# A three-layer feature-interaction kernel on one core: field pairs on partitions in place of transposed products

## The chip, the cores and the metric
The kernel runs on one core of a Trainium2 chip. The metric is device time in microseconds (us) of one execution. A core has TensorE (PE in the profile; its weight loads are PEld), VectorE (DVE), ScalarE (ACT), GpSimd (POOL), SyncE (SP), which here only issues transfers, and 16 DMA engines. Each engine works through its own instructions in order and waits on semaphores that the others raise.

## The reference
A batch of 1024 samples has 39 fields; each field looks up a row of 16 values and a bias, scaled by the sample's feature value. Three interaction layers follow, all per sample b and embedding component d, and then two dense layers on the 624 scaled inputs:

```python
inputs = emb[feature_ids] * feature_vals[:, :, None]          # 1024 x 39 x 16
h = inputs
for i in range(3):
    x = jnp.einsum('bhd,bmd->bhmd', h, inputs).reshape(B, -1, EMB_DIM)
    x = jax.nn.relu(jnp.einsum('bcd,oc->bod', x, Ws[i]) + bs[i][None, :, None])   # 200 outputs
    if i != 2: h, direct = (x[:, :100], x[:, 100:])
    else: direct = x
    finals.append(direct)
cin_result = jnp.sum(jnp.concatenate(finals, axis=1), axis=-1)
d = relu(relu(inputs.reshape(B, -1) @ dnn_W0.T + dnn_b0) @ dnn_W1.T + dnn_b1)    # 624 -> 400 -> 400
out = concatenate((cin_result, d)) @ fc_W.T + fc_b + sum(input_biases)
```

Layer 0 has 780 products per sample and component (symmetric pairs merged), layers 1 and 2 have 100 x 39 = 3900 each.

## The kernel before
The batch is 8 tiles of 128 samples; a tile and one of the 16 components make a chunk, so there are 128 chunks (`CHUNKS`). In a chunk the products of a layer are the contraction of a matmul: 7 tiles of 128 products in layer 0, 31 in layers 1 and 2 each (`KT`). Each value is split into a high part that the one-pass matmul format holds and a low part, and a tile is multiplied as high x (weights high, weights low), 400 columns, and low x (weights high), 200 columns (`multiply_group`, L524 and L525). One group of four tiles in layers 1 and 2 is not split and multiplied in full precision instead (L516).

GpSimd forms the products with samples on the partitions (L397 for layer 0, L414 for layers 1 and 2, 3900 elements in four pieces each). The matmul wants products on the partitions, so every group of four tiles is turned first: TensorE turns those of layer 0 (L496), VectorE transposes blocks of 32x32 for the others (`turn_group`, L719), out of an order of weights and inputs that makes 32x32 blocks enough. ScalarE rounds a turned group to its high part (`high`, L582), VectorE subtracts (`low`, L725), TensorE multiplies. The layer's sum is put together by ScalarE (`low_copy`, L589) and VectorE (`add`, L735), dotted with the final weights (`dot`, L742), and its first 100 outputs are copied, quarter by quarter, as the next layer's h (`quarter`, L598, 16 small ACTIVATEs a layer).

A step i (function `step`, written out by hand; a hardware loop runs over most of them) works on layer 0 of chunk i+1, layer 1 of chunk i and layer 2 of chunk i-1. GpSimd also gathers the embedding rows of the next tile, one indirect DMA for each field (`gather`, L364; two or three at the head of each step, by `gathers(j)`), and scales them once a tile (`scale`, L374 to L385). After the last chunk the dense layers run tile by tile (L530 to L532, L757, L763).

## Time and profile before

| | us |
|---|---|
| median of 3 runs (lowest, highest) | 3019.55 (3016.03, 3020.39) |
| the profiled execution | 3024.12 |
| its span, from first to last instruction | 3022.3 |
| mean granted TensorE clock | 0.996 of full |

Busy shares of the span: PE 95%, PEld 92%, DVE 90%, POOL 80%, ACT 72%. Busy time counts each instruction from start to end, and neighbours on one engine overlap by up to a third, so a share near 90% may still hide idle time: the distance between the starts of two neighbours is what an engine spends on one. A wait is read from the brackets of a row of the timeline: idle time, and what ended it.

### The profile page before, as it was taken

How to read it: one execution, taken by the hardware profiler on the slowest of the kernel's cores; microseconds unless marked ns; L12 is line 12 of the kernel's file. 1: busy time of each engine (PE TensorE's matmuls, PEld its weight loads, DVE VectorE, ACT ScalarE, POOL GpSimd, SP SyncE). 2: the span in 40 equal slices, each digit the busy share in tenths (PEclk: the TensorE clock that was granted, in tenths of full speed). 3: DMA queues.
4: the chain of work that ended last, by engine and by line, in shares of the span. 5: the costliest groups of instructions: out<-in, count | busy, mean ns of one | idle time of the engine just before them, and what ended most of it. 6: DMA issues, size and time to landing. Idle time of an engine off the chain costs nothing.

```text
span 3022.3 us, 69958 instructions
## 1 busy us (share of the span) xinstructions
PE 2883.5 (95%) x18848; PEld 2783.5 (92%) x18848; DVE 2731.5 (90%) x5355; ACT 2163.4 (72%) x6593; POOL 2417.9 (80%) x1513
## 2 busy tenths in 40 slices
PE   0799999999999999999999999999999999999998
PEld 0799999999999999999999999999999999999997
DVE  2699999999999999999999999999999999999995
ACT  2677777777777777777777777777777777777772
POOL 7788888888888888888888888888888888767660
PEclk9899999999999999999999999999999999999999
DMA  6100010000000010000100001000100001000001
GB/s 122 19 1 1 1 22 1 1 1 7 16 1 1 1 22 1 1 1 1 22 1 1 1 1 22 1 1 1 21 2 1 1 1 22 1 0 0 0 35 30
DMA packets 36455, 29.42 MB, mean 10 GB/s; under 512 B 22960, under 2 KB 28976, under 8 KB 36400
## 3 DMA queue, kind: packets, MB, share of 16 engines
q1 hardware_dynamic: 26160, 26.11, 3.8%
q0 software_dynamic: 10240, 2.81, 3.2%
q14 instruction: 48, 0.39, 0.0%
q8 instruction: 7, 0.11, 0.0%
HBM read 26.33 MB, written 2.56 MB: 10 GB/s over the span
## 4 chain that ended last, share of the span: by engine, by line
ACT 30%; issue 29%; DVE 29%; PE 6%; DVEq 2%; ACTq 2%; POOL 2%; DMA 1%; SPq 0%; POOLq 0%
DVE xlo L725 15%; ACT h2q L598 10%; ACT h1q L598 10%; ACT xhi L582 10%; DVE turn L719 7%; DVE acc_sum L735 4%; PE acc L524 2%; DVE x_whole L719 2%; POOL raw L364 1%; DVEq L723 1%; ACTq L580 1%; PE acc L525 1%; DVE spent L742 1%; PE turn L496 1%; PE acc L516 1%
## 5 line engine op out<-in xcount | busy, mean ns | idle before, releaser
L524 PE MATMUL acc<-W,xhi 128*128 128x400 f32 x7808 | 2437.0, 374 | 61.3 <-DVE xlo L725 36.0
L525 PE MATMUL acc<-W,xlo 128*128 128x200 f32 x7808 | 1990.3, 255 | 0.0
L524 PEld LDWEIGHTS acc<-W,xhi 128*128 128x128 f32 x7808 | 1467.5, 188 | 154.5 <-DVE xlo L725 153.5
L725 DVE TENSOR_TENSOR xlo<-turn,xhi 128x512 fp32r<-128x512 f32 (+1 forms) x2088 | 1341.7, 648 | 223.7 <-ACT xhi L582 194.6
L525 PEld LDWEIGHTS acc<-W,xlo 128*128 128x128 f32 x7808 | 1492.1, 191 | 0.0
L582 ACT ACTIVATE xhi<-turn 128x512 fp32r<-128x512 f32 (+1 forms) x2088 | 1165.4, 571 | 397.9 <-PE acc L525 216.2
L414 POOL TENSOR_TENSOR prods<-h1q,xq 128x1092 f32<-128x1092 f32 (+2 forms) x512 | 933.1, 1854 | 413.7 <-ACT h1q L598 407.2
L719 DVE STREAM_TRANSPOSE turn<-prods 128x512 f32<-128x512 f32 (+1 forms) x1792 | 1244.9, 695 | 18.3 <-POOL prods L414 13.3
L414 POOL TENSOR_TENSOR prods<-h2q,xq 128x1092 f32<-128x1092 f32 (+2 forms) x512 | 934.1, 1854 | 12.6 <-ACT h2q L598 12.6
L598 ACT ACTIVATE h1q<-acc_sum 32x25 f32<-32x25 f32 x2048 | 456.2, 223 | 242.5 <-DVE acc_sum L735 215.1
L598 ACT ACTIVATE h2q<-acc_sum 32x25 f32<-32x25 f32 x2048 | 456.9, 223 | 76.9 <-DVE acc_sum L735 49.6
L516 PE MATMUL acc<-w_whole,x_whole 128*128 128x200 f32 x2048 | 393.0, 335 | 0.0
L364 POOL DMA_INDIRECT raw<-table,idx x320 | 313.4, 979 | 89.4 <-issue 82.3
L516 PEld LDWEIGHTS acc<-w_whole,x_whole 128*128 128x128 f32 x2048 | 336.4, 190 | 0.0
L397 POOL TENSOR_TENSOR prods<-xin 128x780 f32 (+1 forms) x128 | 215.5, 1684 | 5.2 <-POOL idx L359 3.1
L496 PE MATMUL turn<-ident,prods 128*128 128x128 f32 (+1 forms) x928 | 146.0, 275 | 69.1 <-POOL prods L397 67.8
L589 ACT ACTIVATE acc_lo<-acc 128x200 f32<-128x200 f32 x384 | 129.2, 337 | 96.7 <-PE acc L525 96.7
L719 DVE STREAM_TRANSPOSE x_whole<-prods 128x512 f32<-128x512 f32 x256 | 177.3, 693 | 0.0
L496 PEld LDWEIGHTS turn<-ident,prods 128*128 128x128 f32 (+1 forms) x928 | 105.6, 141 | 71.7 <-issue 68.3
L735 DVE TENSOR_TENSOR acc_sum<-acc,acc_lo 128x200 f32<-128x200 f32 x384 | 135.2, 352 | 10.4 <-ACT acc_lo L589 10.4
L742 DVE SCALAR_TENSOR_TENSOR spent<-acc_sum,fcp 128x100 f32<-128x100 f32 (+1 forms) x384 | 105.5, 275 | 0.1
L742 DVE DVE_READ_ACCUMULATOR spent<-acc_sum,fcp (+1 forms) x384 | 32.6, 85 | 0.0
(44 smaller groups left out, 227.5 us busy)
## 6 DMA issues: line engine op xcount, KB each, us to landing
xq<-x_store SPq DMA_DIRECT2D x32, 312.0 KB
raw<-table,idx POOLq DMA_INDIRECT x320
prods<-w SPq DMA_DIRECT2D x9, 500.0 KB, 7.8
x_store<-xin SPq DMA_DIRECT2D x8, 312.0 KB
raw<-x_store SPq DMA_DIRECT2D x8, 312.0 KB, 2.9
prods<-d SPq DMA_DIRECT2D x1, 1000.0 KB, 4.8
w_whole<-w SPq DMA_DIRECT2D x2, 400.0 KB, 12.8
prods<-d SPq DMA_DIRECT2D x1, 800.0 KB, 6.5
```

The costliest lines, as they stand in the source:

```text
L364: nc.gpsimd.indirect_dma_start(out=raw[:, m * EMB_COLS:(m + 1) * EMB_COLS], out_offset=None, in_=table, in_offset=bass.IndirectOffsetOnAxi ...
L397: nc.gpsimd.tensor_tensor(prods[:, 0:PAIRS].rearrange("p (s a) -> p s a", a=FIELDS), x[:, 0:FIELDS].unsqueeze(1).broadcast_to([P, SHIFTS, ...
L414: nc.gpsimd.tensor_tensor(out[:, :, a * FIELDS:b * FIELDS].rearrange("p q (h m) -> p q h m", m=FIELDS), hq[layer - 1][:, :, a:b].unsqueeze ...
L496: mm = pe.transpose(turn[slot][0:rows, at:at + P], src[:, t * P:t * P + rows], ident[:])
L516: mm = pe.matmul(bank[:, 0:OUTS], x_whole[:, job - 1, at:at + P], w_whole[:, job - 1, t % GROUP, :], start=False, stop=False, skip_group_c ...
L524: pe.matmul(bank[:, 0:2 * OUTS], hi, w, start=start, stop=end, skip_group_check=True)
L525: mm = pe.matmul(bank[:, 0:OUTS], lo, w[:, 0:OUTS], start=False, stop=end, skip_group_check=True)
L582: op = nc.scalar.activation(xhi[0:rows, slot, cols], turn[slot][0:rows, cols], ACT.Copy)
L598: op = nc.scalar.activation(hq[layer][QUARTER * i:QUARTER * (i + 1), q, :], acc_sum[QUARTER * q:QUARTER * (q + 1), layer, H_QUARTER * i:H_ ...
L719: nc.vector.transpose(place.rearrange("p (t q s) -> p t q s", q=4, s=QUARTER), src.rearrange("p q (t k) -> p t q k", k=QUARTER)).then_inc( ...
L725: op = nc.vector.tensor_tensor(xlo[0:rows, slot, cols], turn[slot][0:rows, cols], xhi[0:rows, slot, cols].bitcast(F32), ALU.subtract)
L735: nc.vector.tensor_tensor(acc_sum[:, layer, :], acc[layer][:, 0:OUTS], acc_lo[:, layer, :], ALU.add).then_inc(s_acc[layer], 1)
```

## The change
Samples move to the columns and products to the partitions, so that no product is transposed. In layers 1 and 2 a tile is one field m (31 of them) with 96 of the h rows on partitions 0 to 95; the remaining 8 fields and 4 h rows fill partitions 96 to 127. SyncE copies the inputs of a chunk out of DRAM onto all partitions that need them (`load_block`, four blocks a chunk; `load_layer0`), and h is turned once a layer by TensorE (`turn`, one 128x128 transpose) and then spread by ScalarE to its places in PSUM (`hrep`, for VectorE) and in SBUF (`hrep_s`, for GpSimd) by six ACTIVATEs (`spread`).

The groups of four tiles of a step are 6 P groups, whose products and low parts are GpSimd's, and 12 D groups, whose products and low parts are VectorE's. ScalarE makes the high parts of both. `ORDER` gives the order in which TensorE multiplies them and ScalarE rounds them. P0 and P1 are layer 0 (4 and 3 tiles), P2, P3 and D0 to D5 are layer 1, P4, P5 and D6 to D11 layer 2; D5 and D11 have three tiles, the last of which holds high and low part in one operand and needs a single 400-column matmul. Both GpSimd and VectorE form the product of the next group just before the subtraction of the present one. Every product tile is split; the full-precision group is gone. GpSimd's gathers stay at the head of its step (`gathers(j)`, ahead of `step`; none at j = 7, where `scale` stands).

Each tile of 128 samples, the scaled inputs are turned by VectorE (`turn_inputs`), stored to DRAM by 8 transfers (`store_inputs`) and copied into further layouts by 22 (`spread_inputs`). The weights are reordered at the start through DRAM (`load_weights`) and split between steps -1, 0 and 1 (`split_weights`). The dense layers read their inputs already turned. The core of the diff:

```diff
+ORDER = [("P", 0), ("D", 0), ("D", 1), ("P", 1), ("D", 2), ("D", 3), ("P", 2), ("D", 4), ("D", 5), ("P", 3),
+         ("D", 6), ("D", 7), ("P", 4), ("D", 8), ("D", 9), ("P", 5), ("D", 10), ("D", 11)]
 LAST = CHUNKS - 1
...
+PRING, DRING, BANKS = 3, 4, 3
...
+def layer_of(kind, g):
+    return g // 2 if kind == "P" else 1 + g // 6
+def tiles_of(kind, g):
+    if kind == "P":
+        return range(GROUP * (g % 2), min(GROUP * (g % 2) + GROUP, KT[0] if g < 2 else KT[1]))
+    return range(2 * GROUP + GROUP * (g % 6), min(3 * GROUP + GROUP * (g % 6), KT[1]))
+def present(i):
+    if not isinstance(i, int):
+        return (0, 1, 2)
+    return tuple(n for n in range(3) if 0 <= i + 1 - n <= LAST)
...
+            def store_inputs(tile):
+                sp.wait_ge(s_xt, tile + 1)
+                waited()
+                for q in range(4):
+                    for j, n in ((0, QUARTER), (1, M_ALL - QUARTER)):
+                        sp.dma_start(
+                            xs[bass.ds(tile * DIM, DIM), QUARTER * j:QUARTER * j + n,
+                               QUARTER * q:QUARTER * (q + 1)].rearrange("d c b -> c d b"),
+                            xt[QUARTER * q:QUARTER * q + n, :, j, :]).then_inc(s_xs, 16)
...
+            def spread_inputs(tile):
+                sp.wait_ge(s_xs, tile * 128 + 128)
+                waited()
+                to = xe[bass.ds(tile * DIM, DIM), :, :, :]
...
+            def step(i, buf):
+                if not isinstance(i, int) or i + 2 <= LAST:
+                    sp.wait_ge(s_prod_p, p_num(i, 1) + 1)
+                    waited()
+                    load_layer0(i + 2)
+                full = 2 in present(i)
+                if full:
+                    sp.wait_ge(s_prod_d, d_num(i, 7) + 1)
+                    waited()
+                load_block(i + 1, buf, 1)
+                if full:
+                    sp.wait_ge(s_prod_d, d_num(i, 9) + 1)
+                    waited()
+                load_block(i + 1, buf, 2)
+                if full:
+                    sp.wait_ge(s_prod_p, p_num(i, 5) + 1)
+                    waited()
+                load_block(i + 1, buf, 0)
+                if full:
+                    sp.wait_ge(s_prod_d, d_num(i, 11) + 1)
+                    waited()
+                load_block(i + 1, buf, 3)
+            load_weights(1, w1)
+            store_inputs(0)
+            spread_inputs(0)
+            load_layer0(0)
...
+            step(1, 0)
+            with sp.Fori(0, TILES - 1) as k:
+                for j in range(DIM):
+                    if j == 9:
+                        store_inputs(k + 1)
+                    if j == 10:
+                        spread_inputs(k + 1)
+                    if j == 12:
+                        sp.wait_ge(s_xe, (k + 2) * (16 * XE_DMAS))
+                        waited()
+                    step(k * DIM + (j + 2), (j + 1) % 2)
...
+            def product(i, par, k):
+                n, layer, tiles = p_num(i, k), layer_of("P", k), tiles_of("P", k)
+                if k == 0:
+                    pool.wait_ge(s_l0x, (i + 2) * 96)
+                elif k == 2:
+                    pool.wait_ge(s_hrep[0], i + 1)
+                    pool.wait_ge(s_xblk[0], (i + 1) * 32)
+                elif k == 4:
+                    pool.wait_ge(s_hrep[1], i)
+                if some(n - 2):
+                    pool.wait_ge(s_lo_p, n - 2)
+                a, count = tiles[0], len(tiles)
...
+            def low(i, k):
+                n, slot, cols = p_num(i, k), p_slot(i, k), len(tiles_of("P", k)) * P
+                pool.wait_ge(s_hi_p, n + 1)
+                nc.gpsimd.tensor_tensor(xlo_p[:, slot, 0:cols], prod_p[:, slot, 0:cols],
+                                        xhi_p[:, slot, 0:cols].bitcast(F32), ALU.subtract).then_inc(s_lo_p, 1)
...
+            def step(i, par, ahead):
+                mine = p_groups(i)
+                for at, k in enumerate(mine):
+                    if at + 1 < len(mine):
+                        product(i, par, mine[at + 1])
+                    elif ahead is not None:
+                        product(i + 1, 1 - par, ahead)
+                    low(i, k)
+            FREE_AT = 7
...
             with pool.Fori(0, TILES - 1) as k:
                 for j in range(DIM):
                     gathers(j)
+                    if j == FREE_AT:
+                        scale(k + 1, True)
                         copy_idx((k + 2) % TILES, k + 3)
+                    step(k * DIM + (j + 2), j % 2, 0)
+            for i in range(2 + DIM * (TILES - 1), CHUNKS):
+                step(i, i % 2, p_groups(i + 1)[0] if i < LAST else None)
+            product(CHUNKS, 0, p_groups(CHUNKS)[0])
+            step(CHUNKS, 0, None)
...
+            def split_tile(bank, hi, lo, w, first, last):
+                pe.matmul(bank[:, 0:2 * OUTS], hi, w, start=first, stop=last, skip_group_check=True)
+                return pe.matmul(bank[:, 0:OUTS], lo, w[:, 0:OUTS], start=False, stop=last, skip_group_check=True)
...
+                    if layer > 0 and t == LAST_T:
+                        mm = pe.matmul(acc[layer][:, 0:2 * OUTS], hi, w, start=start, stop=end,
                                        skip_group_check=True)
...
+                        mm = split_tile(acc[layer], hi, lo, w, start, end)
+                mm.then_inc(done, 1)
...
+            def turn(l, c, i):
+                pe.wait_ge(s_hbuf[l], c + 1)
+                if not isinstance(c, int) or c > 0:
+                    pe.wait_ge(s_prod_d, d_num(i, 5 + 6 * l) + 1)
+                pe.transpose(hrep[l][:, 0, :], hbuf[l][:], ident[:]).then_inc(s_turn[l], 1)
+            def step(i):
+                layers = present(i)
+                if layers == (2,):
+                    turn(1, i - 1, i - 1)
+                for kind, g in step_order(i):
+                    multiply(i, kind, g)
+                    if (kind, g) == ("D", 1) and not (isinstance(i, int) and i < 1):
+                        turn(1, i - 1, i - 1)
+                    if (kind, g) == ("D", 7) and 0 in layers:
+                        turn(0, i + 1, i)
+                if layers == (0,) or layers == (0, 1):
+                    turn(0, i + 1, i)
...
+            def high(i, kind, g):
+                cols = len(tiles_of(kind, g)) * P
+                if kind == "P":
+                    n, slot = p_num(i, g), p_slot(i, g)
+                    act.wait_ge(s_prod_p, n + 1)
+                    if some(n - (PRING - 1)):
+                        act.wait_ge(s_mm_p, n - (PRING - 1))
+                    nc.scalar.activation(xhi_p[:, slot, 0:cols], prod_p[:, slot, 0:cols], ACT.Copy).then_inc(s_hi_p, 1)
+                else:
+                    n, slot = d_num(i, g), d_slot(i, g)
+                    act.wait_ge(s_prod_d, n + 1)
+                    if some(n - (DRING - 1)):
+                        act.wait_ge(s_mm_d, n - (DRING - 1))
+                    nc.scalar.activation(xhi_d[:, slot, 0:cols], prod_d[d_bank(i, g)][:, 0:cols],
+                                         ACT.Copy).then_inc(s_hi_d, 1)
...
+            def take(l, c):
+                act.wait_ge(s_dot[l], c + 1)
+                if some(c):
+                    act.wait_ge(s_turn[l], c)
...
+            def spread(l, c, i):
+                act.wait_ge(s_turn[l], c + 1)
+                if some(c):
+                    act.wait_ge(s_prod_p, p_num(i, 3 + 2 * l) + 1)
+                h = hrep[l][:, 0, :]
+                nc.scalar.activation(hrep[l][0:H_MAIN, 2:4, :],
+                                     h[0:H_MAIN, :].unsqueeze(1).broadcast_to([H_MAIN, 2, P]), ACT.Copy)
+                nc.scalar.activation(hrep[l][H_MAIN:P, 3, :], h[QUARTER:2 * QUARTER, :], ACT.Copy)
+                nc.scalar.activation(hrep_s[l][0:H_MAIN, :], h[0:H_MAIN, :], ACT.Copy)
+                nc.scalar.activation(hrep_s[l][H_MAIN:P, :], h[0:QUARTER, :], ACT.Copy)
+                nc.scalar.activation(hrep[l][H_MAIN:P, 2, :], h[2 * QUARTER:3 * QUARTER, :], ACT.Copy)
+                nc.scalar.activation(hrep[l][0:P - 4, 1, :], h[0:P - 4, :], ACT.Copy).then_inc(s_hrep[l], 1)
+            def step(i):
...
+                for kind, g in step_order(i):
+                    high(i, kind, g)
+                    if (kind, g) == ("D", 2) and 1 in layers and not (isinstance(i, int) and i < 2):
+                        low_copy(2, i - 2, i - 1)
+                    if (kind, g) == ("D", 3) and 1 in layers and inner:
+                        spread(1, i - 1, i - 1)
+                    if (kind, g) == ("D", 4) and 0 in layers:
+                        low_copy(0, i + 1, i)
+                    if (kind, g) == ("P", 3) and layers == (0, 1):
+                        take(0, i + 1)
+                        spread(0, i + 1, i)
+                    if (kind, g) == ("D", 6) and 0 in layers:
+                        take(0, i + 1)
+                    if (kind, g) == ("D", 8) and 1 in layers:
+                        low_copy(1, i, i)
+                    if (kind, g) == ("D", 9) and 0 in layers:
+                        spread(0, i + 1, i)
+                    if (kind, g) == ("D", 10) and 1 in layers:
+                        take(1, i)
+                    if (kind, g) == ("D", 8) and layers == (2,):
...
+            def product(i, par, d):
+                n, layer, tiles = d_num(i, d), layer_of("D", d), tiles_of("D", d)
+                if d % 6 == 0:
+                    dve.wait_ge(s_hrep[layer - 1], i + 2 - layer)
+                if d in (0, 2, 4):
+                    dve.wait_ge(s_xblk[1 + d // 2], (i + 1) * 32)
+                if some(n - (BANKS - 1)):
+                    dve.wait_ge(s_lo_d, n - (BANKS - 1))
+                a, count = tiles[0], len(tiles)
+                to = prod_d[d_bank(i, d)][:, 0:count * P].rearrange("p (t n) -> p t n", n=P)
+                if d % 6 == 5:
+                    h = hrep[layer - 1][:, 1:1 + count, :]
                 else:
...
+            def low(i, d):
+                n, slot, bank = d_num(i, d), d_slot(i, d), prod_d[d_bank(i, d)]
+                count = len(tiles_of("D", d))
+                dve.wait_ge(s_hi_d, n + 1)
+                split = (count - 1 if d % 6 == 5 else count) * P
+                op = nc.vector.tensor_tensor(xlo_d[:, slot, 0:split], bank[:, 0:split],
+                                             xhi_d[:, slot, 0:split].bitcast(F32), ALU.subtract)
+                if d % 6 == 5:
+                    op = nc.vector.tensor_tensor(xhi_d[64:P, slot, split:split + P], bank[0:64, split:split + P],
+                                                 xhi_d[0:64, slot, split:split + P].bitcast(F32), ALU.subtract)
+                op.then_inc(s_lo_d, 1)
...
+            def step(i, par, ahead):
+                layers, mine = present(i), d_groups(i)
+                for at, d in enumerate(mine):
+                    if at + 1 < len(mine):
+                        product(i, par, mine[at + 1])
+                    elif at + 1 - len(mine) < len(ahead):
+                        product(i + 1, 1 - par, ahead[at + 1 - len(mine)])
+                    low(i, d)
+                    if d == 3 and 1 in layers and not (isinstance(i, int) and i < 2):
+                        evacuate(2, i - 2)
+                    if d == 5 and 0 in layers:
+                        evacuate(0, i + 1)
+                    if d == 9 and 1 in layers:
+                        evacuate(1, i)
+                if layers == (0, 1):
+                    evacuate(1, i)
...
```

## Rows read from the trace of the kernel before
**Rows 1.** The page, part 1: busy time, share, count of each engine.
```profile
PE 2883.5 (95%) x18848; PEld 2783.5 (92%) x18848; DVE 2731.5 (90%) x5355; ACT 2163.4 (72%) x6593; POOL 2417.9 (80%) x1513
```
**Rows 2.** Windows: start:end, length, busy (x count) per engine, clock, DMA share, GB/s.
```profile
24.00:28.00 4.00, 0.00 (x0) 0.00 (x0) 2.43 (x3) 1.52 (x3) 3.08 (x4) 1.00 1.00 260
...
1000.00:2000.00 1000.00, 986.97 (x6492) 954.93 (x6490) 936.85 (x1834) 743.45 (x2278) 840.31 (x524) 1.00 0.06 6
```
**Rows 3.** Timeline, ScalarE, one step apart: start, length, instruction, idle before.
```profile
1501.20 0.34 ACT L589 ACTIVATE acc_lo<-acc 128x200 f32<-128x200 f32 x1 [0.28 <-PE acc L525]
...
1523.54 0.34 ACT L589 ACTIVATE acc_lo<-acc 128x200 f32<-128x200 f32 x1 [0.28 <-PE acc L525]
```
**Rows 4.** Timeline, TensorE, a stretch of 15 split tiles without a gap.
```profile
1499.83 0.36 PE L524 MATMUL acc<-W,xhi 128*128 128x400 f32 x1
...
1500.03 0.25 PE L525 MATMUL acc<-W,xlo 128*128 128x200 f32 x1
...
1504.22 0.36 PE L524 MATMUL acc<-W,xhi 128*128 128x400 f32 x1
```
**Rows 5.** Groups of instructions by form: busy us, mean ns | idle before, releaser.
```profile
L414 POOL TENSOR_TENSOR prods<-h1q,xq 128x1092 f32<-128x1092 f32 x256 | 520.0, 2053 | 413.7 <-ACT h1q L598 407.2 <-DMA xq<-x_store 6.5
L516 PE MATMUL acc<-w_whole,x_whole 128*128 128x200 f32 x2048 | 393.0, 335 | 0.0
L397 POOL TENSOR_TENSOR prods<-xin 128x780 f32 x125 | 210.5, 1684 | 4.8 <-POOL idx L359 3.1
L414 POOL TENSOR_TENSOR prods<-h1q,xq 128x780 f32<-128x780 f32 x128 | 194.7, 1521 | 0.0
L374 POOL TENSOR_TENSOR xin<-raw,val 128x624 f32 x7 | 13.1, 1873 | 0.0
```
**Rows 6.** Timeline, TensorE and ScalarE: transposes, and who waited for them.
```profile
1518.64 0.49 PE L496 MATMUL turn<-ident,prods 128*128 128x128 f32 x3
...
1519.24 0.50 ACT L582 ACTIVATE xhi<-turn 128x384 fp32r<-128x384 f32 x1 [0.67 <-PE turn L496]
```
**Rows 7.** Timeline, ScalarE: small and large ACTIVATEs one behind the other.
```profile
1509.14 0.33 ACT L589 ACTIVATE acc_lo<-acc 128x200 f32<-128x200 f32 x1
1509.36 0.61 ACT L582 ACTIVATE xhi<-turn 128x512 fp32r<-128x512 f32 x1
...
1514.84 0.93 ACT L598 ACTIVATE h2q<-acc_sum 32x25 f32<-32x25 f32 x4
1515.79 1.59 ACT L582 ACTIVATE xhi<-turn 128x512 fp32r<-128x512 f32 x3
```
**Rows 8.** Timeline, VectorE and the weight load that waited for it.
```profile
1499.32 0.70 DVE L719 STREAM_TRANSPOSE turn<-prods 128x512 f32<-128x512 f32 x1
1499.92 0.67 DVE L725 TENSOR_TENSOR xlo<-turn,xhi 128x512 fp32r<-128x512 f32 x1
...
1507.71 0.69 DVE L725 TENSOR_TENSOR xlo<-turn,xhi 128x512 fp32r<-128x512 f32 x1 [0.26 <-ACT xhi L582]
...
1508.45 0.19 PEld L524 LDWEIGHTS acc<-W,xhi 128*128 128x128 f32 x1 [0.39 <-DVE xlo L725]
```
**Rows 9.** Timeline, GpSimd: three gathers at the head of a step.
```profile
1501.41 0.99 POOL L364 DMA_INDIRECT raw<-table,idx  x1 [0.15 <-issue]
...
1504.93 1.69 POOL L397 TENSOR_TENSOR prods<-xin 128x780 f32 x1
```
**Rows 10.** Timeline, start: memset, last gather, first product; SyncE's store and reload.
```profile
33.41 0.15 DVE L696 MEMSET prods<- 128x115 f32 x1
...
59.46 0.95 POOL L364 DMA_INDIRECT raw<-table,idx  x1 [0.30 <-issue]
62.54 0.29 POOL L374 TENSOR_TENSOR xin<-raw,val 128x39 f32<-128x39 f32 x1 [2.13 <-DMA raw<-table,idx]
...
386.98 0.56 SPq L312 DMA_DIRECT2D x_store<-xin  x1
395.13 1.75 SPq L317 DMA_DIRECT2D xq<-x_store  x4
```
**Rows 11.** Timeline, TensorE: five dense matmuls apart.
```profile
2972.60 0.34 PE L530 MATMUL acc<-W,xhi 128*128 128x400 f32 x1
...
2973.50 0.34 PE L532 MATMUL acc<-W,xlo 128*128 128x400 f32 x1
```

1024 lines of the change are left out of this document (516 added, 508 removed).

## The prediction, made before the changed kernel was run

> **What bounds the kernel now.** I read the busy shares first, then the windows, then the distance between starts in the timeline, because busy times overlap. The shares [rows 1] put TensorE at 95% and VectorE at 90%, and the window from 1000 to 2000 [rows 2] has TensorE busy for 987 of 1000 us at the full clock. The reader should see there that one stage, the steps, is nearly the whole kernel. One step is 22.34 us: the same ScalarE copy stands at 1501.20 and 1523.54 [rows 3]. What must TensorE do in it? 15 split tiles run from 1499.83 to 1504.22 without a gap, group borders included [rows 4]: 0.293 us a tile, of which the 400-column half takes 0.20. So 61 split tiles are 17.9; the 8 unsplit ones show 2048 records for 1024 tiles, which start every 0.19 us or so (393.0 us busy with overlap [rows 5]), and are 3.1; 7 transposes are about 1.0. That makes 22.0 of 22.3: TensorE bounds the kernel before, with a little idle time left to VectorE. GpSimd, at 80%, has its idle time in one place, behind the copies of h (413.7 us before L414 [rows 5]).
>
> **The change, part by part: TensorE.** It removes the 7 transposes of layer 0 and the unsplit group, and makes the last tile of layers 1 and 2 a single 400-column matmul. A step is then 7 + 30 + 30 = 67 split tiles by 0.293 = 19.6, two halves at 0.20 = 0.4, two h transposes at about 0.2 with their way in and out = 0.4: a floor of 20.4, 1.9 us below the 22.34 of now. 127 such steps would save 240 us. The rest asks whether the others deliver on time.
>
> **VectorE.** The 14 transposes go (L719), 12 products come. A 512-element instruction costs it 0.60 from start to start, transpose and subtraction alike (1499.32 to 1499.92 [rows 8]). 10 products at 0.60, 2 at 0.47, as much for the subtractions, and some 1.7 for three sums and dots: 15.8 of 20.4. The new product reads and writes PSUM, which no row shows; its ends are the 0.60 of the transpose that writes PSUM and twice that, and I take 0.60; at 1.2 VectorE would have 23 us a step and be the bound. With one product ahead instead of two groups, a subtraction may wait for its high part: between product d and subtraction d lie a subtraction and a product, 1.2 us, and the high part takes 0.6. Even 0.3 us of wait at all 12 makes 19.4, still under the floor. I cost it at nothing; its cover is those 4.6 us.
>
> **ScalarE.** 18 roundings, at 0.495 apart (three in 1.59, the last 0.60 long [rows 7]), 3 copies at 0.22, 32 small ACTIVATEs fewer (0.235 apart), and two takes and two spreads of 2 and 6. A spread has one of 256 and five of 128 elements. From 0.22 for 200 and 0.495 for 512 elements the first is 0.28, the others between 0.17 (that slope carried on) and 0.24 (what 25 elements take): I take 0.20, so the next rounding may start 1.28 after a spread begins (1.13 to 1.48). The sum, some 13 us, is no bound. But these instructions stand in line.
>
> **GpSimd.** This is the part with a price. Six products and six subtractions of flat rows, both inputs from SBUF. The two forms of L414 give 191 + 1.705 ns an element (2053 for 1092, 1521 for 780), with one operand standing still for 39 elements; L397, where both run, gives 1684 for 780, that is 191 + 1.914; the strided L374 gives 191 + 2.70 [rows 5]. For 512 elements: 1.06, 1.17 or 1.57; for 384: 0.85, 0.93 or 1.23. Nearest is L397, as both operands run: 1.17 and 0.93. The sum of the step is 13.6, and 39 gathers a tile are 2.44 a step. Gathers cost 1.17 to 1.25 each (three from 1501.41 to 1504.93 with the lead-in [rows 9]: I take 1.22). With `scale` at the one step without a gather (about 4 us: 1.87 for L374 and about as much for the rest and the waits), the mean at the head of a step is 3.2. In all 16.8 of 20.4, which looks hidden. It is not, because of the order.
>
> The Trainium skill, page "GPSIMD Engine Reference", section "Elementwise — side-by-side cycle accounting", puts a two-input instruction at about 2.6 cycles an element because both reads share one port, 4497 ns for 2048; by that, 512 elements are about 1.3 us and the step below 23.2. L397's 2.16 ns an element, its start included, lies near it; L414's 1.88 lies below.
>
> **The chain of a step.** Take S as the start of P0's matmuls, and times from there.
> (a) TensorE does P0, D0, D1 by 3.51; turns h2; ScalarE gets a turned result 0.39 after the last transpose starts (transposes start 0.105 apart at 1518.64, the copy at 1519.24 [rows 6]): 3.90. Spread: +1.28 = 5.18. Rounding of P2, 0.60: 5.78. GpSimd's subtraction: 5.83 to 7.00. TensorE, which finished D3 at 6.93, starts P2 at 7.1: 0.2 lost, the floor is 20.6.
> (b) D4, D5, P3, D6, D7 until 13.77; it turns h1. ScalarE has it at 14.16, and `spread(0)` stands before the rounding of P5. Spread until 15.44, rounding until 16.04, subtraction 16.1 to 17.27. TensorE wants P5 at 17.48: on time, by 0.2.
> (c) But only now can GpSimd go on. Its next instructions are the gathers, 3.2; product P1, 0.93; subtraction P0, 1.17. Done at 22.57, and with semaphore and exposed weight load (start 0.05 behind VectorE's end [rows 8], and about 0.09) TensorE starts the next P0 at 22.7. It had ended D11 at 20.6. So it idles 2.1 us a step, and GpSimd idled 3 to 4 us just before, waiting for P5's rounding. Everything later in the step (P2, P3, P4) has over 0.5 us in hand except (a).
> With gathers the step is 22.7; without them (c) ends at 19.5 and the floor of 20.6 holds. The loop with gathers has 7 x 16 = 112 steps, 15 full steps lie outside it: 2542 + 309 = 2851 us.
>
> **Transfers.** A chunk's inputs are about 2.4 MB a step. At the 260 GB/s that the start shows [rows 2] these are 9 us of transfer in 22.7, each block asked for at least 6 us ahead of use: hidden, at nothing. Half that rate, 19 us, would bring late blocks. The stores of a tile: 2048 runs of 156 bytes took 8.1 us from issue to landing [rows 10], so 3840 runs of 128 bytes are about 13.5, and the copies behind them as much. They are issued five steps before use and delay the next inputs by less than the lead of 8 us or more that those have: nothing.
>
> **Start and end.** Now the last gather ends at 60.4 and its rows are there at 62.5 [rows 10]. After the change VectorE first sets some 4900 elements of constants (0.15 us for 115 [rows 10]; I estimate 5 us, of which 2 delay the gathers): 64. Scaling 3.2, turning 1.2, storing 13.5, copies 13.5, loading: first product at 97. Step -1 exposes a second load and a full hand-over of h: 113. Splitting layer 1's weights, 6200 elements at 1.04 (0.60 - 0.07 for 512): 122. Step 0: 137. Splitting layer 2's: 148 to the effective start of step 1. The end: layer 2 alone, 13 us with its hand-over; then GpSimd's splits of the first dense weights and inputs let TensorE start at 15; 27 matmuls at 0.18 [rows 11] and 4 transposes a tile make 5.6; pipelined over 8 tiles, with sums and store, 64 in all.
> Span: 148 + 2851 + 64 = 3063. The execution profiled now is 1.8 us longer than its span and 4.6 above the median: **3060 us**, 1.3% slower than 3019.55.
>
> **The rivals.**
> A, the forecast: the P5 hand-over followed by the gathers ends last. With 1.06/0.85 and short spreads the step is about 22.2, with 1.3/1.02 and long ones 23.5; start and end 15 us either way. Alone it ranges from 3000 to 3150.
> B, on the other side: TensorE's floor decides. GpSimd's lead survives, the gathers lie in its idle 3 to 4 us, and the steps are 20.6: 148 + 127 x 20.6 + 64 = 2828, median 2825. For it: every engine's sum is under 17 us a step, and TensorE bounds now. Against: P5's subtraction cannot precede `spread(0)`, and after it 5.3 us of GpSimd stand against 3.3 us of TensorE. It needs that span to be short by 2.0 us; from 0.4 us short on (22.3 a step) the change is faster, and between the two lie times from 2825 to 3010.
> C, GpSimd at the strided rate: +0.4 on each of P2, P5 and P0 and +0.3 on P1's product, 24.2 a step: 3060 + 112 x 1.5 + 15 x 0.4 = 3234. For it: L374. Against: flat rows, and L397.
> D, transfers or PSUM: inputs at half the rate, or products at 1.2 us, make 23 to 25 a step in all 127: 3150 to 3350. For it: nothing moves this much in the steps before (6 GB/s [rows 2]). Against: the 260 GB/s.
> That one product ahead starves the subtraction, so that VectorE ends last, belongs to D's price and I give it next to nothing.
>
> **How the numbers follow.** A 0.55, B with all between 0.25, C 0.12, D 0.08. Around 3019.55, 0.2% (6 us) is what a measurement can tell from no change. A lies with 0.05 below 3013.5 and 0.06 within; so faster 0.30, same 0.07, slower 0.63. Range: 2930 to 3200 leaves out half of B and nearly all of C above 3200. The forecast's own range is 3000 to 3150.
>
> **What would show it.** In the profile after: TensorE idle once a step before P0's first matmul, released by GpSimd's `xlo_p`, about 2 us, shorter by 1.2 in steps with two gathers and near zero in the last 14; a small gap before P2; GpSimd idle 3 us before P5's subtraction, released by ScalarE; steps of 22.7 and then 20.6; GpSimd's 512-element instructions at 1.17. The forecast is wrong if TensorE's gap stands before a D group (VectorE or the blocks late), if steps in the gather loop are as short as the last 14, or if the first step starts later than 160.

## The result and the profile after

The changed kernel takes 3434.95 us (median of three, 3423.92 to 3442.47), against 3019.55: a ratio of 1.137, with a 95% interval from 1.133 to 1.141. The forecast was 3060 us within 2930 to 3200. Slower was right, and so was the place of the largest gap; the size was not: 41 us forecast, 415 measured. The profiled execution took 3423.92 us, its span is 3422.1.

From the page of the kernel after, part 1 [rows 1], and below it the window from 1000 to 2000 us [rows 2]:

```profile
PE 2848.0 (83%) x17912; PEld 2748.2 (80%) x17912; DVE 2144.5 (63%) x4563; ACT 1851.2 (54%) x4774; POOL 2232.9 (65%) x1921
```

```profile
1000.00:2000.00 1000.00, 855.22 (x5455) 825.28 (x5454) 646.89 (x1385) 560.91 (x1461) 677.25 (x583) 0.96 0.40 104
```

No engine is full any more. TensorE was busy for 987 of 1000 us and is now busy for 855, at a mean granted clock of 0.96; no other engine took over as the bound by its sum. Such a page says that the order of the work decides, and the waits say where. This is the view of waits of the kernel after (engine, output, line <- releaser: total us, times, longest):

```profile
POOL xlo_p L530 <- ACT xhi_p L732: 927.9, 252, 12.4
...
PE acc L606 <- POOL xlo_p L530: 558.1, 366, 113.0
```

The second row is the one that costs: 366 times in 128 steps, nearly three a step, TensorE waits for a subtraction of GpSimd, which itself waited for ScalarE's rounding (first row). The timeline of TensorE, only its rows behind a gap, shows the three places:

```profile
1503.61 0.45 PE L606 MATMUL acc<-W,xhi_p 128*128 128x400 f32 x1 [0.33 <-POOL xlo_p L530]
1508.33 0.45 PE L606 MATMUL acc<-W,xhi_p 128*128 128x400 f32 x1 [1.34 <-POOL xlo_p L530]
1516.11 0.46 PE L606 MATMUL acc<-W,xhi_p 128*128 128x400 f32 x1 [0.69 <-POOL xlo_p L530]
1526.93 0.45 PE L606 MATMUL acc<-W,xhi_p 128*128 128x400 f32 x1 [0.33 <-POOL xlo_p L530]
1532.86 0.70 PE L606 MATMUL acc<-W,xhi_p 128*128 128x400 f32 x1 [2.55 <-POOL xlo_p L530]
```

In order: before P5, before the next P0 (a step with two gathers), before P2, before P5 again, and before the P0 after it (three gathers). These are the prediction's three hand-overs: (b) before P5, (c) before P0, (a) before P2. The row behind the gap before P0, in GpSimd's timeline:

```profile
1502.26 1.29 POOL L530 TENSOR_TENSOR xlo_p<-prod_p,xhi_p 128x512 fp32r<-128x512 f32 x1 [3.24 <-ACT xhi_p L732]
1503.70 0.99 POOL L484 DMA_INDIRECT raw<-table,idx  x1
1504.99 0.94 POOL L484 DMA_INDIRECT raw<-table,idx  x1 [0.30 <-issue]
1505.95 1.02 POOL L524 TENSOR_TENSOR prod_p<-l0x 128x384 f32<-128x384 f32 x1
1506.92 1.27 POOL L530 TENSOR_TENSOR xlo_p<-prod_p,xhi_p 128x512 fp32r<-128x512 f32 x1
```

GpSimd stands idle for 3.24 us, then does P5's subtraction, and only behind it two gathers, P1's product and P0's subtraction, which TensorE waits for until 1508.33.

Lengths of a step below are distances between the first ACTIVATEs of `spread(1)` of two steps. The loop's 112 steps repeat in sixteens: six have two gathers, nine have three, one has none and `scale`. Two of the nine have columns of their own, since one more thing delays them. The columns: median step with two gathers; with three (the other seven); the three-gather step behind `spread_inputs`; the first one after the loops of GpSimd and VectorE turn back to their start (`turn`); the mean of the 112; the last steps, which have no gathers; start of `spread(1)` in step 1; median time; ratio to before with its interval.

```
kernel                 2 gath  3 gath  behind  turn   mean   last   start   time      ratio
after                  23.31   26.11   27.78   30.81  25.40  21.70  176.3   3434.95   1.137 [1.133, 1.141]
e1_gathers_moved       21.71   22.11   31.46   24.16  23.09  21.70  172.0   3160.66   1.048 [1.046, 1.049]
e2_round_first         21.13   21.29   28.89   25.57  22.12  21.13  170.6   3040.86   1.008 [1.007, 1.010]
e3_fill                23.31   24.54   27.48   30.64  24.89  22.83  169.0   3372.47   1.118 [1.116, 1.120]
e4_two_ahead           23.31   26.10   24.82   29.14  25.21  21.70  172.6   3382.32   1.121 [1.119, 1.122]
e5_all                 20.24   21.46   32.24   22.05  21.81  20.18  173.1   2993.25   0.991 [0.989, 0.993]
e6_issues_apart        23.30   26.12   24.54   31.20  25.33  21.70  172.5   3404.72   1.127 [1.125, 1.130]
e7_all_apart           20.23   21.46   21.46   21.85  21.14  20.18  180.7   2926.19   0.969 [0.968, 0.971]
e8_no_gathers          21.70   21.70   26.75   25.69  22.50  21.70  172.5   3086.12   1.022 [1.020, 1.023]
e9_placed              20.18   20.23   20.22   21.98  20.44  20.18  170.6   2841.29   0.941 [0.940, 0.942]
e10_placed_start       20.18   20.23   20.23   22.13  20.48  20.18  163.7   2830.39   0.938 [0.936, 0.939]
e11_placed_two_ahead   20.18   20.18   20.18   21.21  20.35  20.18  173.5   2829.26   0.937 [0.936, 0.938]
e12_best               20.18   20.18   20.18   21.12  20.34  20.18  161.2   2820.52   0.934 [0.933, 0.936]
```

### The profile page after: what moved, and what is told of

It reads as the page before. It is cut to its first block, busy times and chain, and to the rows that moved or that the text cites. A ratio compares the mean times of both kernels' runs of the same rounds, so it can differ in the third digit from the quotient of the medians.

```text
span 3422.1 us, 66460 instructions
## 1 busy us (share of the span) xinstructions
PE 2848.0 (83%) x17912; PEld 2748.2 (80%) x17912; DVE 2144.5 (63%) x4563; ACT 1851.2 (54%) x4774; POOL 2232.9 (65%) x1921
## 4 chain that ended last, share of the span: by engine, by line
issue 46%; POOL 34%; PE 7%; SPq 7%; DVE 3%; DMA 2%; ACT 1%; POOLq 1%; DVEq 0%; ACTq 0%
POOL prod_p L524 16%; POOL xlo_p L530 12%; POOL raw L484 5%; PE acc L606 4%; SPq L351 3%; PE acc L607 2%; DMA xrep<-xs 1%; DMA l0x<-xs 1%; DVE xlo_d L923 1%; DVE prod_d L915 1%; SPq L291 1%; POOL xin L497 0%; SPq L314 0%; SPq L301 0%; SPq L367 0%
## 5 line engine op out<-in xcount | busy, mean ns | idle before, releaser
L606 PE MATMUL acc<-W,xhi_d 128*128 128x400 f32 x5632 | 1779.8, 375 | 7.1 <-DVE xlo_d L923 7.1
L923 DVE TENSOR_TENSOR xlo_d<-prod_d,xhi_d 128x512 fp32r<-128x512 f32 (+1 forms) x1536 | 983.1, 640 | 1008.2 <-ACT xhi_d L738 1004.0
L530 POOL TENSOR_TENSOR xlo_p<-prod_p,xhi_p 128x512 fp32r<-128x512 f32 (+1 forms) x768 | 952.7, 1240 | 927.9 <-ACT xhi_p L732 927.9
L606 PE MATMUL acc<-W,xhi_p 128*128 128x400 f32 x2944 | 1004.0, 391 | 558.1 <-POOL xlo_p L530 558.1
L607 PE MATMUL acc<-W,xlo_d 128*128 128x200 f32 x5632 | 1466.7, 260 | 0.0
L607 PEld LDWEIGHTS acc<-W,xlo_d 128*128 128x128 f32 x5632 | 1119.5, 199 | 0.0
L606 PEld LDWEIGHTS acc<-W,xhi_d 128*128 128x128 f32 x5632 | 1102.2, 196 | 9.3 <-DVE xlo_d L923 8.1
L915 DVE TENSOR_TENSOR prod_d<-hrep,xrep 128x512 f32<-128x512 f32 (+1 forms) x1536 | 1025.6, 668 | 38.9 <-DMA xrep<-xs 25.5
L738 ACT ACTIVATE xhi_d<-prod_d 128x512 fp32r<-128x512 f32 (+1 forms) x1536 | 885.9, 577 | 260.6 <-DVE prod_d L915 176.6
L607 PE MATMUL acc<-W,xlo_p 128*128 128x200 f32 x2944 | 769.5, 261 | 0.0
L628 PE MATMUL acc<-W,xhi_d 128*128 128x400 f32 x256 | 93.3, 364 | 0.0
```

Source lines behind the costliest of these rows:

```text
L530: nc.gpsimd.tensor_tensor(xlo_p[:, slot, 0:cols], prod_p[:, slot, 0:cols], xhi_p[:, slot, 0:cols].bitcast(F32), ALU.subtract).then_inc(s_l ...
L606: pe.matmul(bank[:, 0:2 * OUTS], hi, w, start=first, stop=last, skip_group_check=True)
L607: return pe.matmul(bank[:, 0:OUTS], lo, w[:, 0:OUTS], start=False, stop=last, skip_group_check=True)
L738: nc.scalar.activation(xhi_d[:, slot, 0:cols], prod_d[d_bank(i, g)][:, 0:cols], ACT.Copy).then_inc(s_hi_d, 1)
L915: nc.vector.tensor_tensor(to, h, xrep[:, (par + layer - 1) % 2, a:a + count, :], ALU.mult).then_inc(s_prod_d, 1)
L923: op = nc.vector.tensor_tensor(xlo_d[:, slot, 0:split], bank[:, 0:split], xhi_d[:, slot, 0:split].bitcast(F32), ALU.subtract)
```

## The experiments

All start from the changed kernel. Four questions, in the order in which they came up. Comments behind # in the diffs are added here. Step lengths come from the one execution of each kernel that was profiled, times are medians; two executions of the changed kernel differ by up to 19 us, with the mean granted clock between 0.947 and 0.955.

**1. Is the row "P5's rounding, gathers, product, subtraction" what ends last?**

`e1_gathers_moved`: the gathers go from the head of the step, where they stand behind P5's late subtraction, to the idle time ahead of it.

```diff
-                    gathers(j)                      # head of step j
...
                     elif ahead is not None:
                         product(i + 1, 1 - par, ahead)
+                        if fill is not None:
+                            gathers(fill)           # ahead of low(i, 5)
```

> Only the place of the gathers changes: from the head of GpSimd's step to just behind the product of the next P0, where it waits 3.2 us for P5's rounding. Theory 1 (order: the gathers stand on the chain P5 - P1's product - P0's subtraction): the 112 steps with gathers fall from 25.4 to about 21.8, the length of the last steps, the half-clock stretches vanish (granted clock from 0.955 to 0.99), total about 3030 (3000 to 3070). Rival 2 (load: GpSimd and the transfers have too much to do, wherever it stands): same work, same time, within 1% of 3435. Rival 3 (one product ahead starves VectorE): no change either.

Measured: 3160.66 us. Steps with two gathers fall from 23.31 to 21.71, with three from 26.11 (24.54 where the clock did not fall) to 22.11. 274 us of the 415 come back by moving 39 instructions a tile, none taken away. Ordinary steps are as expected; the total is some 130 us above the expectation, because the steps that come once a tile did not shrink with them: `scale` still takes 26.4, the step behind `spread_inputs` now 31.46.

`e2_round_first`: ScalarE rounds P5 before the six ACTIVATEs of `spread(0)` instead of behind them.

```diff
-                    if (kind, g) == ("D", 9) and 0 in layers:
+                    if (kind, g) == ("P", 5) and 0 in layers:
                         spread(0, i + 1, i)
```

> Only ScalarE's order changes: P5 is rounded before the spread of h1, not after it. Theory 1: GpSimd gets P5 some 3 us earlier, the gathers fall into what was its wait, P5's own 0.33 us gap on TensorE goes too; steps about 21.4, total about 2990 (2950 to 3060), the clock at 0.99. Rivals 2 and 3: within 1% of 3435, as the work is the same. If the spread's end itself (products of D0 and P2 of the next step) were the limit, this would be slower than the changed kernel.

Measured: 3040.86 us, 21.13 and 21.29 a step. One moved condition is worth 394 us. In ordinary steps P5's wait and P0's wait are both gone; what is left of TensorE's gaps is P2's alone:

```profile
1501.17 0.45 PE L606 MATMUL acc<-W,xhi_p 128*128 128x400 f32 x1 [0.70 <-POOL xlo_p L530]
1522.31 0.45 PE L606 MATMUL acc<-W,xhi_p 128*128 128x400 f32 x1 [0.70 <-POOL xlo_p L530]
1543.60 0.45 PE L606 MATMUL acc<-W,xhi_p 128*128 128x400 f32 x1 [0.69 <-POOL xlo_p L530]
```

`e8_no_gathers`: the other end of the same dose. No gather in the loop, nor of the second tile before it. It leaves out the rows of all tiles but the first, so its output is not that of the reference.

```diff
-            pool.wait_ge(s_gather, tile * (16 * FIELDS) + 16 * FIELDS)
+            pool.wait_ge(s_gather, 16 * FIELDS)
...
-                    gathers(j)
```

> The kernel after without the gathers in the loop (the rows of the first tile are used for every tile; all arithmetic is kept). Theory (the gathers lie in the row that ends last): ordinary steps fall to the 21.7 us of the last 14 steps, which have none, TensorE's gap in front of P0 and the stretches at half clock go; once a tile 6 us more for late blocks: span 172 + 112 x 22.1 + 331 + 74 = 3050, between 3030 and 3075. The forecast's own arithmetic would give 20.6 us for such steps, a span of 2900 to 2940. Rival (the gathers' reads only disturb the transfers, and half clock has another cause): steps above 23, span above 3150.

Measured: 3086.12 us. Ordinary steps are 21.70, exactly the last steps of the kernel after. So a step of the kernel after is 20.18 (the step in which TensorE never waits, `e9_placed`), plus 1.52 for the gaps before P2 and P5 (0.69 and 0.33, and 0.25 behind each: the weight load's row shows an idle time longer by that than the matmul's), plus 1.61 for two gathers or 2.84 for three. That closes for P0 as well: 1.34 + 0.25 is 1.59, 2.55 + 0.25 is 2.80. The forecast's arithmetic gave 20.6 without gathers and is 1.1 off there. The span came out 42 us above the expectation: a tile's `scale` step (26.4), the one behind `spread_inputs` (26.8) and the turn (25.7) each cost more than I had counted.

`e5_all`: gathers moved, and both roundings (P5 and P2) ahead of their spreads.

```diff
-                    if (kind, g) == ("D", 3) and 1 in layers and inner:
+                    if (kind, g) == ("P", 2) and 1 in layers and inner:
                         spread(1, i - 1, i - 1)
```

> Both reorderings together: the gathers stand behind the product of the next P0 instead of at the head of the step, and ScalarE rounds P5 before spread(0) and P2 before spread(1). Theory (the step ends with ScalarE's rounding of P5, GpSimd's gathers, product and subtraction in a row; each 1.3 us taken out of that row shortens the step until TensorE's own 20.4 to 20.6 us is reached): ordinary steps of 20.5 to 20.8 us instead of 21.2 (rounding first) and 21.9 (gathers moved), TensorE without the gap of 0.69 us before P2; span 2930 to 2970. Rival (VectorE, which then gets its spread 0.6 us later, takes over as the one waited for): steps of 21.2 us and more, TensorE's gap in front of D4 or D10, span near 3020.

Measured: 2993.25 us, 0.9% below the kernel before. Steps with two gathers are 20.24. Those with three stay at 21.46. That is a length the rival allowed (21.2 and more), but not its place: TensorE's only gap stands before P0, not before a D group, and is 1.03, since three gathers no longer fit between P0's product and the moment P5's rounding is there. The span missed the expectation by 23 us, by these steps and by one that now takes 32.24, which is question 3.

**2. Does the lowered clock count?** After a gap of 2.55 us before P0, in steps with three gathers, the granted clock often falls; in the 42 steps with two gathers, whose gap is 1.34, it never did. The timeline of TensorE in the kernel after, and windows over the same place:

```profile
246.21 0.70 PE L606 MATMUL acc<-W,xhi_p 128*128 128x400 f32 x1 [2.56 <-POOL xlo_p L530]
246.70 0.37 PE L607 MATMUL acc<-W,xlo_p 128*128 128x200 f32 x1
246.87 0.58 PE L606 MATMUL acc<-W,xhi_p 128*128 128x400 f32 x1
247.25 0.37 PE L607 MATMUL acc<-W,xlo_p 128*128 128x200 f32 x1
247.42 0.58 PE L606 MATMUL acc<-W,xhi_p 128*128 128x400 f32 x1
```

```profile
246.00:250.00 4.00, 3.79 (x14) 3.78 (x15) 3.02 (x7) 0.69 (x2) 3.50 (x4) 0.50 0.41 120
250.00:254.00 4.00, 4.00 (x21) 3.98 (x20) 0.00 (x0) 0.79 (x3) 0.00 (x0) 0.67 0.00 0
```

A split tile takes 0.55 instead of the 0.293 of [rows 4], at a clock of 0.50, the 1.2 GHz level. A three-gather step without it is 24.54; with it 26.1 or 27.4. In all, the clock stood at the lower level for 268 us of the 112 steps.

`e3_fill`: ten matmuls that nobody reads, behind D11, so that TensorE works through most of the gap.

```diff
+                if not isinstance(i, int):
+                    for _ in range(10):
+                        pe.matmul(acc[1][:, 2 * OUTS:512], W[:, 0:P], W[:, 0:512 - 2 * OUTS], start=True, stop=True)
```

> Adds ten matmuls of 112 columns that nobody reads behind D11 in the looped steps, into free columns of a PSUM bank; nothing else changes. It tells the two parts of the loss apart. If the half-clock stretches cost what the trace suggests (25.4 a step measured against 24.1 from the steps without them, 1.3 x 112 = 140 us), keeping TensorE busy over most of its idle time gives up to that back, less some 15 us where the added work outlasts the wait: about 3310 (3280 to 3400), granted clock back to 0.98 or more. If the clock is only a sign of the wait and costs nothing, since the chain runs over GpSimd: 3435 or somewhat more.

Measured: 3372.47 us, 62 less than the kernel after, although the last steps became 1.13 longer. Of the 112 steps 41 now take 24.5, where 17 did, and 27 take 26 and more, where 52 did. The lower clock covers 123 us of them in place of 268, and their sum falls by 57. So the clock is worth at least 60 us of the 415. Since `e3_fill` took away only about half of the low stretches, I estimate 105 for all of them, by proportion (57 x 268 / 145); no run shows the whole. And it is a follower: in `e2_round_first` ordinary steps need no cure, because the gap is gone.

**3. Transfers at nothing?** In `e2_round_first`, and in every kernel up to here, the step behind `spread_inputs`, one of 16, was some us longer than its neighbours. SyncE's queue there, and GpSimd's product that waited:

```profile
1110.00 16.01 SPq L351 DMA_DIRECT2D xe<-xs  x20
1126.27 0.57 SPq L353 DMA_DIRECT2D xe<-xs  x1
...
1128.02 0.34 SPq L367 DMA_DIRECT2D l0x<-xs  x1
...
1130.91 0.32 SPq L379 DMA_DIRECT2D xrep<-xs  x1
```

```profile
1133.07 1.26 POOL L524 TENSOR_TENSOR prod_p<-l0x 128x512 f32<-128x512 f32 x1 [7.30 <-DMA l0x<-xs]
```

Twenty issues hold the queue for 16.01 us, 0.8 each, where a load takes 0.32; the loads of the next step stand behind them. Meanwhile the DMA engines' share was 0.66 over the first 5 us and 0.27 to 0.29 over the rest. The prediction counted the DMA engines' bytes and not the queue's time.

`e6_issues_apart`: the same twenty issues, two behind each load over two steps.

```diff
-                    if j == 10:
-                        spread_inputs(k + 1)
...
+                load_block(i + 1, buf, 1)
+                more(1)                  # two of the twenty, where j is 10 or 11
```

> The kernel after with one edit on SyncE's queue: the 20 DMA issues of spread_inputs no longer stand in one piece of 16 us before the loads of one step, but two behind each load, over two steps. Same bytes, same transfers. Theory (the queue that issues is what delays the blocks once a tile, at 0.8 us an issue, not the transfers): the step that now takes 27 to 31 us takes 24.5 to 26, seven times 3 to 5 us: 3435 becomes 3395 to 3415. Rival (the DMA engines are the limit, so that the blocks come late wherever the issues stand): no change, or the lateness spread over two steps, 3430 to 3445.

Measured: 3404.72 us. The step behind `spread_inputs` falls from 27.78 to 24.54 (26.0 where the clock fell), like its neighbours. Same bytes, so it was the queue. The total is 30 us less. In the executions profiled the seven steps give 21 of that; the rest is not above what the clock and the start vary by. It is more in the kernel with both reorderings, whose shorter steps give the queue less time:

> Both reorderings, the 20 issues of spread_inputs two behind each load, and at the start the first inputs of layer 0 and three blocks loaded before spread_inputs(0). Theory: start of step 1 at about 155 us instead of 168 to 172, 112 gather steps of 20.6 to 20.9 with about 4 us more once a tile where GpSimd's loop turns, 15 others of 20.6, tail 73: span 2870 to 2900. Rival (late blocks come from the transfers, not from the issuing queue): the once-a-tile step stays near 28 us and the span is above 2925.

`e7_all_apart` adds this edit to `e5_all`, and loads the first inputs and three blocks ahead of the first `spread_inputs`. Measured: 2926.19 us, 67 less than `e5_all`; the step behind `spread_inputs` is 21.46 instead of 32.24. The loop is as expected but for the three-gather steps, and the span is 24 us above the expectation. The start got worse (180.7 instead of 173.1): the first inputs were loaded earlier, but GpSimd was busy with 24 gathers of the second tile until 100.4, and the layer-0 inputs of step 1 still stand behind the issues of layer 2's weights, which now end at 148.6 (143.4 in the kernel after). GpSimd waits 21.57 us for them.

`e4_two_ahead` asks for the other thing in the change's description: VectorE's products two groups ahead.

```diff
-                    if at + 1 < len(mine):
-                        product(i, par, mine[at + 1])
+                    if at + 2 < len(mine):
+                        product(i, par, mine[at + 2])
```

> VectorE's products are formed two groups ahead of the subtraction in place of one; all else as in the changed kernel. Theory 1: VectorE's 8 us of waiting a step is slack behind ScalarE, which waits for h on TensorE; no change, 3420 to 3450. Rival 3 (one ahead starves the subtraction): steps fall by the waits of the subtraction, 1 to 3 us each, total 3050 to 3300.

Measured: 3382.32 us, 52 less, which neither theory gave. Ordinary steps with two gathers and the last steps are the same to 0.01 us; the step behind `spread_inputs` is 24.82 instead of 27.78, the first one after the turn 29.14 instead of 30.81. These thirteen steps give 30 us, about what the two profiled executions differ by. The other 22 go with a mean granted clock of 0.958 to 0.965 in place of 0.947 to 0.955; why it was higher is open. In ordinary steps the second product ahead gives nothing; it is a cushion for steps in which something comes late.

**4. Is TensorE's floor within reach?** GpSimd has a second idle stretch, 2.0 us before P4's product, where it waits for h2. `e9_placed` puts one gather of each step there; it is otherwise `e7_all_apart` with the start of the kernel after.

```diff
                     low(i, k)
+                    if k == 2 and fill is not None:
+                        gathers(fill, 0, 1)         # the first; the rest behind the next P0's product
```

> Both reorderings and SyncE's issues apart as in e7_all_apart, the start as in the kernel after, and of the two or three gathers of a step one stands behind the subtraction of P2, where GpSimd waits 2.0 us for h2, and the others behind the product of the next P0. Theory (with three gathers the row P0's product, gathers, P5's subtraction, P1's product, P0's subtraction is 1.0 us late for TensorE, with two it is not): the steps of 21.46 us become 20.23 like the others, some 60 of 112, so 75 us less than e7_all_apart, and 8 less by the start: a span of 2835 to 2850. Rival (GpSimd is simply full in a step with three gathers, or the gather in the middle delays P3): 21.2 us and more stay, span above 2900.

Measured: 2841.29 us. Every ordinary step is 20.18 to 20.23. The page's first row and the window from 1000 to 2000 us of `e9_placed`, and GpSimd's two idle stretches with a gather in each:

```profile
PE 2655.2 (94%) x17912; PEld 2641.0 (93%) x17912; DVE 2134.2 (75%) x4563; ACT 1876.5 (66%) x4774; POOL 2261.7 (80%) x1924
```

```profile
1000.00:2000.00 1000.00, 988.71 (x6727) 985.77 (x6726) 795.73 (x1710) 701.97 (x1801) 843.81 (x716) 1.00 0.51 130
```

```profile
1515.36 0.99 POOL L502 DMA_INDIRECT raw<-table,idx  x1
1516.81 1.30 POOL L542 TENSOR_TENSOR prod_p<-hrep_s,xrep 128x512 f32<-128x512 f32 x1 [0.46 <-ACT hrep L794]
...
1524.51 0.99 POOL L502 DMA_INDIRECT raw<-table,idx  x1
1525.80 0.95 POOL L502 DMA_INDIRECT raw<-table,idx  x1 [0.30 <-issue]
1526.76 1.29 POOL L548 TENSOR_TENSOR xlo_p<-prod_p,xhi_p 128x512 fp32r<-128x512 f32 x1
```

`e10_placed_start` reorders the start (inputs of layer 0 ahead of `spread_inputs(0)` and of layer 2's weights; the second tile's gathers in three lots), `e11_placed_two_ahead` and `e12_best` add the second product ahead.

```diff
+            load_layer0(0)
...
             spread_inputs(0)
-            load_layer0(0)
...
+            load_layer0(2)
             load_weights(2, w2)
-            load_layer0(2)
```

> e9_placed with the order of the start changed on SyncE (first inputs of layer 0 and three blocks ahead of spread_inputs(0), the layer-0 inputs of step 1 ahead of the weights of layer 2) and on GpSimd (the gathers of the second tile in three lots instead of one of 30 us). Theory (the start is set by SyncE's queue of issues and by those gathers): spread(1) of step 1 begins at 150 to 160 us instead of 172 to 176, 12 to 22 us less than e9_placed. Rival (the start is set by the weights' arrival and split): within 5 us of e9_placed, or later as in e7_all_apart.

Measured: 2830.39 us, 11 less than `e9_placed`. The first spread of all starts at 107.7 instead of 123.2, but the one of step 1 at 163.7 instead of 170.6: half of the gain is given back. The trace shows eight gathers, the last of the three lots, between P3's subtraction (129.20) and P1's product (140.38) of GpSimd there; no run moves them.

> e9_placed with VectorE's products formed two groups ahead of the subtraction instead of one. Theory (one ahead costs only where blocks come late, since VectorE has idle time in every step and the high part is there in 0.6 us): ordinary steps the same within 0.05 us, the total 0 to 15 us below e9_placed. Rival (one group ahead starves the subtraction at a length of step near TensorE's floor): steps shorter by 0.2 us and more, 25 us and more in all.

Measured: 2829.26 us, 12 less than `e9_placed` (the ranges, 2827.7 to 2831.1 and 2838.3 to 2844.6, do not touch). Steps with two gathers are 20.18 in both, those with three 20.18 instead of 20.23; the gain lies mostly in the first step after the turn (21.21 instead of 21.98), the rest in the `scale` step and the three-gather steps.

> e10_placed_start with VectorE's products two groups ahead: the last two edits together. Theory (they act in different places, the start and the steps with late blocks, so their gains add: 5 to 11 us by the start, 8 to 12 by two ahead, from e9_placed's 2841): 2815 to 2826, TensorE's own floor of 20.18 us in nearly all of the 112 steps. Rival (the gains overlap, or VectorE's two products ahead hold the later start back): no less than 2829.

Measured: 2820.52 us, ratio 0.934 [0.933, 0.936]: the gains add, and this is the fastest version, 6.6% below the kernel before and 18% below the changed kernel, with the changed kernel's instructions in another order and, on VectorE, one more product ahead.

## Why the prediction was wrong

The mechanism was right in part: the sign, the chain, its releaser, its place before P0, the shorter gap with two gathers, the small gap before P2, GpSimd's 3 us of idle time before P5's subtraction. The step that failed is the pricing of that chain and of what hangs on it. The terms in (a) and (b) were too small, above all ScalarE's spread, 1.28 forecast and 1.73 measured: ordinary steps became 24.08 in the mean and not 22.7, 154 us. And four things stood at nothing: the clock behind the gap, SyncE's queue, the loop's turn, and gathers that stand still in single steps, with the `scale` steps 148 us. The prediction's own sign of being wrong, a first step later than 160, also came true: it starts at 172.4.

The sum against the execution profiled, with the forecast's own parts. Its S_1 is the spread's start less 3.9.

```
                         forecast   measured
start of step 1            148        172.4     +24
112 steps with gathers   2542       2844.7     +302   (22.7 -> 25.40 each)
15 other steps            309        331       +22   (13 at 21.7, one at 28.6, one without layer 0 at 20.6)
tail                       64         73.7     +10
```

Of the 302 us in the loop, 154 are ordinary steps that are wider than 22.7 (42 at 23.31 and 70 at 24.54 if the clock holds); 63 are ordinary steps in which it did not; 36 are the six turns of the loop inside the stretch, 25 the seven steps behind `spread_inputs`, 12 the `scale` steps, and 12 two single steps. These are worked out from the step lengths. The clock's part is larger than the 63: a `scale` step takes 24.79 where it held and 26.2 and more where it did not, and it was low in all six steps after a turn as well. `e3_fill` gave back 57 in the loop, `e6_issues_apart` 21 in the steps behind `spread_inputs`.

- **ScalarE, the spread at 1.28.** The mis-sized term that counts most. Its six ACTIVATEs, in the timeline of ScalarE after:

```profile
1523.14 0.36 ACT L768 ACTIVATE hrep<-hrep 96x256 f32<-96x256 f32 x1 [1.63 <-PE hrep L639]
1523.51 0.25 ACT L770 ACTIVATE hrep<-hrep 32x128 f32<-32x128 f32 x1
1523.77 0.27 ACT L771 ACTIVATE hrep_s<-hrep 96x128 f32<-96x128 f32 x1
...
1524.87 0.63 ACT L732 ACTIVATE xhi_p<-prod_p 128x512 fp32r<-128x512 f32 x1
```

  It takes 1.73: 0.37 and five of 0.27. The four 25-element copies of [rows 7] were already 0.235 apart, and a 200-element copy 0.22; the prediction took 0.20, a value below both. Even its upper end, 1.48 for the spread, is 0.25 short. The spread comes twice in the chain, so 0.9 us a step.
- **GpSimd at 1.17.** Measured 1.27 to 1.31, starts 1.25 apart, and 1.02 for 384. L397 was the nearest row taken; the strided 1.57 was too high and L397's 1.17 was 0.1 too low. Four such instructions stand in (a), (b) and (c), some 0.4 us. The Trainium skill ("GPSIMD Engine Reference", section "Elementwise — side-by-side cycle accounting") has about 2.6 cycles an element. The trace agrees with that: from 384 to 512 elements an instruction grows by some 0.27 us, 2.1 ns an element. The "about 1.3" that the prediction reads from the page also holds the 0.19 us start of [rows 5]; the page's 4497 ns for 2048 alone would give an estimate of 1.1 to 1.2.
- **(a), 0.2 lost.** 0.69, and 0.25 more behind it for the weight load. **(b), on time by 0.2.** Late by 0.33, and 0.25 behind that. From P0's first matmul to P5's subtraction are 17.25 us (1508.33 to 1525.58), forecast 16.1; from there to the next P0 7.28 with three gathers and 6.07 with two, a mean of 6.8 where 6.6 was forecast. So (c), the part with the large loss, was sized nearly right, and the two that were called small or harmless carry the error. With a margin of 0.2 us after four estimated terms, "on time" was not a finding.
- **TensorE's floor.** 20.4 forecast, 20.18 measured in steps in which it never waits. Right, and on the good side.
- **VectorE.** Right: 646.89 of 1000 us are 16.4 a step, forecast 15.8 (the prediction's own terms add up to 15.6), and the page has TensorE wait 7.1 us for it in the whole run. "I cost it at nothing" holds in ordinary steps (`e4_two_ahead`: no change to 0.01 us); in those behind `spread_inputs` and after a turn it cost some 30 us.
- **"Transfers: nothing."** Wrong, though no block was late by bandwidth: the mean share is 0.40. The step that failed priced the DMAs as bytes and left out what they cost on the queue that issues them.
- **No term for the clock, none for the loop's turn.** At least 63 and 36 us. In the steps of the kernel before the clock stands at 1.00 [rows 2], so no row pointed at the first; but a gap of 2.1 us a step was forecast, and the question what a gap does to the clock was not asked.
- **Start and tail.** First product at 109.3, forecast 97. The prediction had stores, copies and loads in a row but not their issues: the first `spread_inputs` holds the queue for 15.2 us from 87.60 on, with the layer-0 load behind it. The 28.6 us step lies among the last ones: GpSimd stands still for 9.38 us before a product, without a releaser, and for 7.0 to 9.6 in every version here; its cause is open. The first product:

```profile
109.32 2.22 POOL L524 TENSOR_TENSOR prod_p<-l0x 128x512 f32<-128x512 f32 x2 [9.82 <-DMA l0x<-xs]
```

- **Rival B** had nearly the time of another order: 2825 us for steps at TensorE's floor. `e12_best` is that case, 2820.52. That they are so close is in part luck: its steps are 20.33 in the mean and not 20.6, 34 us less in 127, and its start and end are some 21 us longer than forecast. The prediction named what B needed, a span 2.0 us shorter between P5's subtraction and P0's; `e2_round_first` leaves that span and lets it start earlier, by the 1.73 of the spread.
- **The range.** A alone was given 3000 to 3150 with "1.3/1.02 and long ones 23.5" as the upper end. The mean of the ordinary steps with the clock held is 24.08, and 25.40 with all the rest: the widths of the terms were too narrow by 0.6, and the fall of the clock behind the gap, the held queue and the turn were not in them.

## What to carry to other kernels

Where two engines hand over in both directions each step, write down what stands in line between them on either engine, and put instructions that nobody waits for soon (here the gathers and the spread) into the idle time ahead of the hand-over, not behind it: the same instructions in another order run from 3435 to 2821 us here. Price a block of DMA issues as time on its queue, and ask what is queued behind. Where a margin is smaller than the error of the terms under it, forecast with both signs, and where the forecast contains an idle stretch of TensorE, ask what the granted clock does behind it.
